# Mixture-of-experts stage: per-tile gathers by slot lists built on TensorE, in place of 64 row scatters

## What is computed

```python
logits = xf @ router_w.T                          # 8 experts
scores = jax.nn.softmax(logits, axis=-1)
topk_scores, topk_ids = jax.lax.top_k(scores, 2)
topk_scores = topk_scores / topk_scores.sum(-1, keepdims=True)
# for each expert e, weighted with the token's share of it:
h = silu(x @ w_gate[e]) * (x @ w_up[e])           # 128 -> 512
y = h @ w_down[e]                                 # 512 -> 128
```

## Time and profile before

| | us |
|---|---|
| three executions | 2059.76, 2061.23, 2064.73 |
| median | 2061.23 |
| the profiled execution, its own time | 2063.71 |
| its span, first to last instruction | 2061.9 |
| PE busy, share of the span | 1301.8, 63% |
| DVE busy | 1045.1, 51% |
| ACT busy | 642.5, 31% |
| POOL busy | 526.5, 26% |
| first MoE phase, about | 793 to 1238 |
| second MoE phase, about | 1608 to the end |

### The profile page before, as it was taken

One profiled execution on the slowest core, in us unless ns is written; L12 is line 12 of the kernel. 1 busy time (PEld: TensorE's weight loads), 2 busy tenths in 40 slices (PEclk: granted clock), 3 DMA queues, 4 the chain that ended last, 5 costly groups with the idle time before them and its releaser, 6 DMA issues.

```text
span 2061.9 us, 34069 instructions
## 1 busy us (share of the span) xinstructions
PE 1301.8 (63%) x10601; PEld 852.2 (41%) x10602; DVE 1045.1 (51%) x2359; ACT 642.5 (31%) x1132; POOL 526.5 (26%) x584
## 2 busy tenths in 40 slices
PE   1566367777756565008999933888887401999891
PEld 0444245445434445005555511555554400555550
DVE  5777455666636773522222255767674442222225
ACT  1222034444443221003333310555555100333330
POOL 1334111111103340472222212212210065222220
PEclk9877578989988875559999975999999555999995
DMA  8500021121200000011111156333231011111114
GB/s 235 66 0 0 16 48 33 36 44 31 38 11 0 0 0 0 30 53 32 34 36 36 35 133 103 55 52 60 45 62 23 0 40 48 35 35 36 35 36 131
DMA packets 194423, 89.80 MB, mean 44 GB/s; under 512 B 128939, under 2 KB 186676, under 8 KB 194356
## 3 DMA queue, kind: packets, MB, share of 16 engines
q1 hardware_dynamic: 185652, 71.02, 17.0%
q0 software_dynamic: 8704, 17.91, 2.4%
HBM read 28.96 MB, written 30.03 MB: 29 GB/s over the span
## 4 chain that ended last, share of the span: by engine, by line
PE 42%; DVE 11%; issue 9%; POOL 9%; DMA 7%; SPq 6%; ACT 1%; DVEq 1%; POOLq 0%; ACTq 0%
PE PS L913 13%; PE PS L939 7%; POOL slots L1127 5%; DMA qT<-qs 5%; SPq L811 4%; PE PS L580 3%; PE PS L929 3%; PE PS L501 2%; PE PS L549 2%; PE PS L307 2%; PE PS L565 2%; SPq L1282 1%; POOL ks L767 1%; PE PS L537 1%; PE PS L878 1%
## 5 line engine op out<-in xcount | busy, mean ns | idle before, releaser
L913 PE MATMUL PS<-wgu,xTs 128*128 x584 | 306.3, 608 | 25.7 <-issue 24.6
L639 ACT ACTIVATE pt<-PS 128x768 f32<-128x768 f32 (+1 forms) x256 | 234.2, 918 | 257.5 <-PE PS L501 256.2
L1020 DVE TENSOR_TENSOR pt<-pt,PS 128x512 f32<-128x512 f32 x146 | 100.5, 688 | 338.6 <-PE PS L913 305.6
L1132 POOL DMA_INDIRECT outs<-ys,xs x144 | 137.9, 957 | 418.3 <-DVE ys L1028 412.1
L720 DVE TENSOR_REDUCE m<-PS 128x4 f32<-128x1024 f32 x128 | 156.2, 1224 | 95.2 <-PE PS L501 93.9
L720 DVE TENSOR_REDUCE sg<-PS 128x6 f32<-128x768 f32 x128 | 122.1, 955 | 128.8 <-PE PS L501 127.5
L501 PE MATMUL PS<-tables 64*128 64x192 bf16 (+2 forms) x2048 | 184.6, 260 | 0.0
L965 ACT ACTIVATE pt<-PS 128x512 f32<-128x512 f32 x146 | 87.2, 597 | 294.7 <-PE PS L913 294.7
L939 PE MATMUL PS<-wdn,pt 128*128 x1152 | 163.5, 285 | 21.4 <-issue 19.6
L1127 POOL DMA_INDIRECT slots<-xr,ix x128 | 122.8, 960 | 209.8 <-DVE ix L1011 188.5
L939 PEld LDWEIGHTS PS<-wdn,pt 128*128 128x128 f32 x1152 | 139.4, 191 | 79.7 <-issue 79.6
(11 more groups left out here) (196 smaller groups left out, 2298.5 us busy)
## 6 DMA issues: line engine op xcount, KB each, us to landing
slots<-empty SPq DMA_DIRECT2D x38, 258.0 KB, 9.9
xs<-slots SPq DMA_DIRECT2D x152, 64.5 KB, 1.8
pt<-outs SPq DMA_DIRECT2D x16, 512.0 KB, 4.2
outs<-ys,xs POOLq DMA_INDIRECT x144, 2.2
wgu<-in_L_ffn_w_gate SPq DMA_DIRECT2D x1, 2048.0 KB
wgu<-in_L_ffn_w_up SPq DMA_DIRECT2D x1, 2048.0 KB
wdn<-in_L_ffn_w_down SPq DMA_DIRECT2D x8, 256.0 KB
qT<-hqT SPq DMA_DIRECT2D x128, 4.0 KB
```

The lines of the kernel that those rows point to most:

```text
L639: s.activation(k.pt[:, a % 4, :, 0:w], k.PS[:, self.bank:self.bank + 2, 0:w], ACT.Exp, scale=self.scale).then_inc(self.s_p, 1)
L913: t.matmul(k.PS[:, 1 + 2 * p + w, :], k.xTs[:, p, :], k.wgu[:, w, ds(e, 1), :].squeeze(1), start=True, stop=True).then_inc((self.s_gate_ps ...
L1020: v.tensor_tensor(k.hs[:, p, :], k.sgs[:, p, :], k.PS[:, 2 + 2 * p, :], ALU.mult).then_inc(self.s_h, 1)
L1132: g.indirect_dma_start(k.outs, bass.IndirectOffsetOnAxis(ap=k.xs[:, u, D:D + 1].bitcast(I32), axis=0), k.ys[:, u, :], None).then_inc(self. ...
```

## The change

- The logits stage has a buffer for each of the 8 groups (`xng`, in memory of the attention's qT and kT) and four for the transposes; all logits lie in one PSUM bank, and the route reads them there. The copy L990 is gone, and the loops are written out.
- SP stores the normalised tokens group by group in a DRAM tensor `rows`, behind 256 rows that serve the unused slots.
- The slot number of each pair is split into tile `qa` and place `qb`. For each of the 64 columns of pairs (32 tiles, two experts each) DVE writes three one-hot tables in bf16: `hotb` (128 columns, equal to the place) and two halves of `hota` (76 columns each, equal to the tile, times the token's tile number or its place). PE multiplies them, all 64 products accumulated in one bank: the result is, for each slot, the token's row number.
- From this DVE makes the lists `dst` and `src` (four instructions), one column for each tile of slots.
- The 64 scatters, the table `slots`, its 38 filling DMAs and the loads of `xs` by SP are gone. POOL gathers each tile from `rows` by `src` and scatters its result to `outs` by `dst`.

```diff
@@ Moe.tensor
-        with eng.Fori(0, NG // 2 - 1) as m:
-            for u in range(2):
-                transposes(2 * m + u + 1, 1 - u)
-                logits(2 * m + u, u)
...
+        transposes(0)
+        transposes(1)
+        for g in range(NG):
+            if g + 2 < NG:
+                transposes(g + 2)
+            logits(g)
...
+        for g in range(NG):
+            eng.wait_ge(self.s_hot, g + 1)
+            for i in range(2 * GT):
+                last = t.matmul(k.PS[:, 7, 0:2 * NL], k.hotb[:, g % 2, i, :], k.hota[:, g % 2, i, :],
+                                start=g + i == 0, stop=g == NG - 1 and i == 2 * GT - 1, skip_group_check=True)
+            last.then_inc(self.s_list_ps, 1)
@@ Moe.vector
-        def rows(m):
-            for u in range(RING):
-                t = RING * m + u
-                if not isinstance(m, int):
-                    eng.wait_ge(self.s_sc[u], self.sc0 + 32 * m)
-                for r in range(2):
-                    normalise(k, t, k.xr[:, u, r, 0:D])
-                v.tensor_copy(k.xr[:, u, :, D].bitcast(I32), k.dest[:, :, ds(t, 1)].squeeze(2))
-                v.tensor_copy(k.ix[:, u, :], k.pos[:, :, ds(t, 1)].squeeze(2)).then_inc(self.s_row, 1)
...
+        for g in range(NG):
             for j in range(GT):
-                last = normalise(k, g * GT + j, k.xn4[:, u, j, :])
+                last = normalise(k, g * GT + j, k.xng[g][:, j, :])
             last.then_inc(self.s_xn, 1)
+        eng.wait_ge(self.s_lg_ps, NG)
+        self.route(eng, ch)
+
+        def hot(g, u):
+            if not isinstance(g, int):
+                eng.wait_ge(self.s_list_ps, g - 1)
+            for j in range(GT):
+                for r in range(2):
+                    i, at = 2 * j + r, ds(g * GT + j, 1)
+                    v.tensor_scalar(k.hotb[:, u, i, :], k.iotab[:, :], k.qb[:, r, at], None, ALU.is_equal)
+                    v.tensor_scalar(k.hota[:, u, i, 0:NL], k.iotab[:, 0:NL], k.qa[:, r, at],
+                                    k.lists[:, ds(g * GT + (j + 2), 1)], ALU.is_equal, ALU.mult)
+                    last = v.tensor_scalar(k.hota[:, u, i, NL:2 * NL], k.iotab[:, 0:NL], k.qa[:, r, at],
+                                           k.lists[:, P + NL + r:P + NL + r + 1], ALU.is_equal, ALU.mult)
+            last.then_inc(self.s_hot, 1)
+        hot(0, 0)
+        hot(1, 1)
+        with eng.Fori(1, NG // 2) as m:
             for u in range(2):
+                hot(2 * m + u, u)
+        eng.wait_ge(self.s_list_ps, NG)
+        ch.run(v.tensor_copy(k.low_part[:, :], k.PS[:, 7, NL:2 * NL]))
+        ch.run(v.scalar_tensor_tensor(k.row[:, :], k.PS[:, 7, 0:NL], 2.0 * P, k.low_part[:, :], ALU.mult, ALU.add))
+        ch.run(v.tensor_tensor(k.dst[:, :], k.row[:, :], k.lists[:, P:P + NL], ALU.max))
+        v.tensor_scalar(k.src[:, :], k.dst[:, :], 1, None, ALU.logical_shift_right).then_inc(self.s_list, 1)
@@ Moe.route
-        ch.run(v.tensor_copy(k.pos[:, :, :], k.top[:, :, :]))
+        ch.run(v.tensor_scalar(k.qa[:, :, :], k.top[:, :, :], 1.0 / P, -(0.5 - 1.0 / 256), ALU.mult, ALU.add))
+        ch.run(v.tensor_scalar(k.qa[:, :, :], k.qa[:, :, :], ROUND, None, ALU.add))
+        ch.run(v.tensor_scalar(k.qa[:, :, :], k.qa[:, :, :], ROUND, None, ALU.subtract))
+        ch.run(v.scalar_tensor_tensor(k.qb[:, :, :], k.qa[:, :, :], -1.0 * P, k.top[:, :, :], ALU.mult, ALU.add))
@@ Moe.gpsimd
-                g.indirect_dma_start(k.slots, bass.IndirectOffsetOnAxis(ap=k.ix[:, u, r:r + 1], axis=0),
-                                     k.xr[:, u, r, :], None).then_inc(self.s_sc[u], 16)
+        eng.wait_ge(self.s_list, 1)
+
+        def gather(i):
+            g.indirect_dma_start(k.xs[:, i % RING, :], None, k.rows[:, :],
+                                 bass.IndirectOffsetOnAxis(ap=k.src[:, i:i + 1], axis=0)).then_inc(self.s_ld[i % RING], 16)
+        for i in range(RING):
+            gather(i)
         for i in range(NS):
             u = i % RING
+            eng.wait_ge(self.s_xT_ps, i + 1)
+            gather(i + RING)
             eng.wait_ge(self.s_y, i + 1 + CR)
-            g.indirect_dma_start(k.outs, bass.IndirectOffsetOnAxis(ap=k.xs[:, u, D:D + 1].bitcast(I32), axis=0),
+            g.indirect_dma_start(k.outs, bass.IndirectOffsetOnAxis(ap=k.dst[:, i:i + 1], axis=0),
                                  k.ys[:, u, :], None).then_inc(self.s_st[u], 16)
```

More of the change, by code:

```diff
@@ L42 @@
 NG = NT // GT
-DR = D + 1
 RING = 4
@@ L856, in __init__ @@
         self.s_added = k.sem(name + "_added")
-        self.sc0, self.ga0 = run * 32 * (NT // RING), run * 16 * (NG // RING)
+        self.s_stored = k.sem(name + "_stored")
         self.ld0, self.st0 = run * 16 * (NS // RING + 1), run * 16 * (NS // RING)
-        self.s_sc = [k.sem(f"moe_scattered_{i}") for i in range(RING)]
+        self.ga0 = run * 16 * (NG // RING)
         self.s_ld = [k.sem(f"moe_loaded_{i}") for i in range(RING)]
@@ L946, in scalar @@
         k, s = self.k, self.k.nc.scalar
-        with eng.Fori(0, NG // 2) as m:
-            for u in range(2):
-                eng.wait_ge(self.s_xnT_ps, 2 * m + u + 1)
-                s.activation(k.xnTg[:, u, :], k.PS[:, u, :], ACT.Copy).then_inc(self.s_xnT, 1)
+        for g in range(NG):
+            eng.wait_ge(self.s_xnT_ps, g + 1)
+            if g >= 4:
+                eng.wait_ge(self.s_lg_ps, g - 3)
+            s.activation(k.xnTg[g % 4], k.PS[:, g % 4, :], ACT.Copy).then_inc(self.s_xnT, 1)
         eng.wait_ge(self.s_lg, 1)
@@ L1012, in vector @@
-        rows(0)
-        with eng.Fori(1, NT // RING) as m:
-            rows(m)
+        eng.wait_ge(self.s_lg_ps, NG)
[12 more added lines that the diff above has]
+            last.then_inc(self.s_hot, 1)
@@ L1053, in bc @@
             return x.unsqueeze(2).broadcast_to([P, NT, NE])
-        ch.run(v.tensor_reduce(k.mx[:, :], lg, AX.X, ALU.max))
-        v.tensor_tensor(lg, lg, bc(k.mx[:, :]), ALU.subtract).then_inc(self.s_lg, 1)
+        logits = k.PS[:, 4, 0:NT * NE].rearrange("p (t e) -> p t e", e=NE)
+        ch.run(v.tensor_reduce(k.mx[:, :], logits, AX.X, ALU.max))
+        v.tensor_tensor(lg, logits, bc(k.mx[:, :]), ALU.subtract).then_inc(self.s_lg, 1)
         eng.wait_ge(self.s_e, 1)
@@ L1223, in __init__ @@
         self.eidf, self.eid = sb("eidf", [1, NS + 2]), sb("eid", [1, NS + 2], I32)
-        self.pos, self.ix = sb("pos", [P, 2, NT], I32), sb("ix", [P, RING, 2], I32)
-        self.xr, self.dest = sb("xr", [P, RING, 2, DR]), sb("dest", [P, 2, NT], I32)
-        self.xs, self.ys = sb("xs", [P, RING, DR]), sb("ys", [P, RING, D])
+        self.lists, self.iotab = sb("lists", [P, P + NL + 2]), sb("iotab", [P, P], BF16)
+        self.qa, self.qb = sb("qa", [P, 2, NT]), sb("qb", [P, 2, NT])
+        self.low_part, self.row = sb("low_part", [P, NL]), sb("row", [P, NL])
+        self.dst, self.src = sb("dst", [P, NL], I32), sb("src", [P, NL], I32)
+        hot = self.pt[:, 0:3].rearrange("p a b c -> p (a b c)").bitcast(BF16)
+        self.hotb = hot[:, 0:2 * 2 * GT * P].rearrange("p (u i c) -> p u i c", u=2, c=P)
+        self.hota = hot[:, 2 * 2 * GT * P:2 * 2 * GT * (P + 2 * NL)].rearrange("p (u i c) -> p u i c", u=2, c=2 * NL)
+        self.xs, self.ys = sb("xs", [P, RING, D]), sb("ys", [P, RING, D])
         self.yr = self.pt[:, :, :, :].rearrange("p u a (b r d) -> p u (a b) r d", r=2, d=D)
@@ L1229, in __init__ @@
         self.sgs, self.hs, self.hTs = (self.pt[:, i, :, :] for i in range(3))
-        self.empty = sb("empty", [P, RING * DR])
-        self.slots = nc.dram_tensor("slots", ((NS + RING) * P, DR), F32, kind="Internal").ap()
+        self.rows = nc.dram_tensor("rows", ((2 + NT) * P, D), F32, kind="Internal").ap()
         self.outs = nc.dram_tensor("outs", ((2 * NT + RING) * P, D), F32, kind="Internal").ap()
@@ L1316, in _ @@
             assert n == NW_FIRST + NW_LOADS, n
-            sp.dma_start(k.empty[:, :], a["empty"]).then_inc(s_zero, 16)
-            sp.wait_ge(s_zero, 16)
-            empty_slots()
+            sp.wait_ge(s_w, 16 * NW_FIRST)
+            for i in range(2):
+                sp.dma_start(k.rows[i * P:(i + 1) * P, :], k.ident[:, :]).then_inc(s_pad, 16)
             sp.wait_ge(s_w2, 16 * NW_LOADS)
```

104 lines of the change are left out of this document (39 added, 65 removed).

## The result

The changed kernel takes 1924.9 us, the median of four executions (1918.64 to 1928.9). The kernel before, executed on the same chip, takes 2061.82 us (2059.76 to 2064.73). The ratio is 0.9332, with a 95% interval of 0.9300 to 0.9364. The profiled execution is the fastest of the four, 1918.64 us, with a span of 1916.8.

The account below looks back on a forecast made before the run. Bounds by MoE stage: a ring of waits (logits), POOL (scatters), mostly busy PE with waits (experts). 14 − 0.5 + 41 + 10 = 64.5 us a phase, 130.3 with both phases and fillings; forecast median 1931 us, range 1910 to 1975.

Parts of the forecast that it names:

- logits: MoE logits stage: cutting the ring of waits makes PE the bound and gains 14 us a phase, between 10 and 20.
- route: MoE route: four instructions replace L1115, +0.7 us, and the copy L990 goes, −0.2 us; sum +0.5 us a phase.
- first table to first down product: From the end of the route to the experts: 45 us in place of 86, a gain of 41 us a phase.
- expert loop: MoE expert loop: the wait for the load goes, 10 us gained a phase; the turn stays at 4.5 us.
- Tables: DVE's one-hot tables: 64 times three instructions, 34.2 to 41.9 us a phase, taken as 38.
- Rival 1: One-hot instructions are slow, 0.26 us each or 50 us for the tables: +12 us a phase, 1955 us; chance 0.15.
- Last products, lists, first gathers: Between tables and experts: PE's last list products 2 us with hand-over, DVE's lists 1.1, first gather to PE's transpose 2.8.
- The wait: Expert loop: the load's wait for an earlier result goes, interval 3.8 to 3.25 us, 18 × 0.57 = 10 us.
- Fillings: The 19 fillings after the first MoE hold SP while ks is ready: 1.3 us gained once; those at the start nothing.
- 2 (the loop gains nothing): Expert loop gains nothing because the uneven interval is the register load's: +20 us, 1951 us; chance 0.17.
- 3 (late gathers): Expert loop gathers arrive late and the kernel is slower: sign turns at 10.8 us landing, 2121 us at 12; chance 0.02.
- rival 4: Expert loop: the gather waits behind the scatter, POOL paces tiles at 4.0 us, 24 us a phase: 1979 us; chance 0.04.

Follow-up runs that it names:

- experiment 5: Changed kernel with the one-hot tables compared from the fp32 numbers instead of their bf16 copy; 1937.61 us, ratio 0.9392 to the kernel before.
- experiment 3: Changed kernel with every fourth tile's gather held back until the result of the tile four before has landed; 1996.94 us, ratio 0.9702 to the kernel before.
- experiment 4: Changed kernel with every gather of tile i+4 issued behind the scatter of tile i, without a wait for landing; 1933.78 us, ratio 0.9388 to the kernel before.
- experiment 2: Kernel before with two `slots` tables, both filled at the start, so no filling follows the first MoE; 2055.76 us, ratio 0.9989.

## Why the prediction was right, point by point

For one MoE phase, first and second, in us:

| step | predicted | measured |
|---|---|---|
| logits | −14 | −13.8, −11.2 |
| route | +0.5 | +0.7, +0.7 |
| first table to first down product | −41 | −42.5, −42.0 |
| expert loop, 71 intervals | −10 | −14.2, −15.5 |
| last down product to the end | 0 | −0.6, −1.0 |
| sum | −64.5 | −70.4, −69.0 |

- **Logits.** DVE's 32 normalisations took 8.25 us (8.3 forecast), PE became the bound, and a group took 2.46 us at 0.50 and 1.28 at 1.00. The value between the two clocks was right for the first MoE and too good for the second; as it was a choice between two ends, the hit in the first is partly luck. The reason given for it, that the clock rises because PE works without a gap, is only half right. In the second MoE PE worked 11.2 of 12 us and the clock stayed at 0.50. The rule that I weighed (the Trainium skill, TensorE: Matmul & The Clock Gate, Part 1), full clock for an engine that has been kept busy, is therefore not borne out by this stage on its own.
- **Tables.** 37.3 us measured, 38 forecast. The estimate of 37 us by the tier table of the Trainium skill, VectorE: DVE Perf Modes, agrees with the measurement, and so did its 0.16 and 0.21 us for each instruction. Rival 1, 0.26 us each, did not happen; experiment 5 shows that an fp32 source alone adds 4.8 of the rival's 12 us.
- **Last products, lists, first gathers.** 1.2, 1.0, and 0.9 + 2.8 us in place of 2.2, 1.1 and 2.8: the products were cheaper, POOL's start dearer (0.9 us, not 0.3). The two errors cancel, 5.9 us against 6.1, which is luck. The kernel before shows such a start too: its first scatter begins at 845.67, 0.97 us after the slot numbers are copied. The second tile came 1.1 us after the first.
- **Expert loop.** The step that was mis-sized: 10 us forecast, 14.2 and 15.5 measured, a mean interval of 3.51 and 3.49 us where the forecast is 3.56 (three of 3.25 and one of 4.5). The wait went as forecast: 3.84 to 3.24 us, 18 × 0.60 = 10.8. The other 3 to 5 us come mainly from the turn, 4.50 to 4.34 (first MoE) and 4.53 to 4.27 us (second), which I had said the change leaves alone. It is no accident of one profile: the turn takes 4.47 to 4.53 us in the three kernels with SP's loads, and 4.23 to 4.34 us in the kernels with gathers and four tiles a turn. L941's idle time at the turn fell from 0.70 to 0.54 us in the first MoE and 0.44 in the second (medians). As two register loads stand there behind the wait for `xs`, the earlier gather is the likely cause; it fits experiments 3 and 4, where a later gather lengthens just this idle time, but the turn was not isolated.
- **Fillings.** 1.3 us forecast, 1.24 us seen at the start of attention; experiment 2 finds no measurable difference in the total.
- **Rivals.** 2 (the loop gains nothing) is refuted by the intervals, and experiment 3, with the chain in the trace of the kernel before, shows the wait as their cause. 3 (late gathers) had its mechanism right: experiment 3 makes one in four late and takes back 70 of the 139 us. The gathers land after 2.5 us, far from the 10.8 at which the sign would turn. (Both this working and that of rival 4 take 3.8 us for the old mean interval; the four of the earlier trace rows average 3.70, which gives 10.5 us here, and some 8 us a phase more for rival 4.) 4 (POOL paces the tile) is refuted by POOL's waits of 1 to 2 us for the next result.
- **Total.** For the two phases 129 us were forecast, and 139 are measured in the profiled executions: 10 more from the loop (7 of them its turn), 2 to 3 more from the way to the first down product, 1 to 2 more at the end of the phases, 3 less from the logits, nearly all in the second phase. The changed kernel's profiled execution is 6 us below its median, so the median fell by 137 us where 130 were forecast: 1924.9 against 1931. That the medians agree better than the phases do, 6 us against 10, comes from the other phases, and is luck.

## What to carry to other kernels

When scatters of single rows pace a stage, one can compute the inverse list with one-hot products and gather instead: 64 POOL issues at 1.27 us became DVE work of 0.59 us a column, and the next bound is the number of small DVE instructions, which another engine can share. A load that reuses a buffer should be issued ahead of the work that waits for a result and not behind it; being late cost its lateness and 0.4 us more here, for which the register loads behind it are the likely reason, not an isolated one. Reading which interval of an unrolled loop is long, by position, tells a wait from the turn of the loop before anything is changed.
